# The start of a graph-attention kernel: first rows of h from centred x, first chunk of adj in halves, second group of x inside the units

## The chip, the cores and the metric

The kernel runs on one core of one Trainium2 chip. The metric is device time in microseconds (us), the median of three runs. TensorE is PE in the profile, VectorE is DVE, ScalarE is ACT, GpSimd is POOL and SyncE is SP.

## What is computed

x is 8192 x 128, adj is 8192 x 8192 with zeros and ones, both float32; alpha is 0.5 and beta is 1.

```python
h = jnp.maximum(_layernorm(x, axis=-1), 0.0)
deg = jnp.clip(adj.sum(axis=1), 1.0)
dis = deg ** (-0.5)
diffusion = (dis[:, None] * adj * dis[None, :]) @ h - h
norms = jnp.maximum(jnp.linalg.norm(h, axis=-1), COS_EPS)
sim = h @ h.T / (norms[:, None] * norms[None, :])
attn = jax.nn.softmax(beta * sim * adj, axis=1)
out = x + diffusion + jax.nn.sigmoid(alpha) * (attn @ h - h)
```

## The kernel before

The 8192 rows are 64 tiles of 128. Four groups of 16 tiles (g = 0 to 3) hold x, and later h in its place, in SBUF (`x_st`). The output rows are eight panels of 1024. A unit is one tile of columns against one panel: 512 units, in chunks of 16. For each unit n:

- `cosines(n)` on PE: six matmuls of 512 columns over the halves `uT_hi` and `uT_lo` of the transposed unit rows, into one of two PSUM slots;
- `masked(n)` on DVE (line 718): times the 0/1 bytes of the transposed adj;
- two exponentials on ACT: a half-precision head `ehi` (line 432) and the float32 `ef` (line 436);
- `rest(n)` on POOL (line 339): the tail `elo`;
- `sums(n)` on PE, three units behind (`LAG`): 24 matmuls of 128 or 129 columns.

adj comes from HBM by POOL's queue, cast from float32 to 8 bits on the way: a chunk is four transfers of 32 partitions, each of 1024 rows of 512 elements (2 KB read, 512 B written). Three buffers hold chunks. `turn(m)` (DVE, line 647) transposes a quarter of a chunk, four units' worth, and SP stores the result to HBM for the last stage; `turn(m)` for m >= 4 reuses the place of `turn(m-4)` and is called in unit 4m-3. So chunk 1 is first needed in unit 13, between `masked(13)` and `masked(14)`, and the third quarter of chunk 0 in unit 5.

Ahead of the units: groups 0 and 1 of x are loaded by SP and ACT, then mean and variance of group 0 (`stats_of_x`, `early_var`), a rough reciprocal root on ACT from the float's bits and three Newton steps on DVE (`early_shift`), 16 relu activations on ACT that make h, the squares of h (`stats_of_h`, `square_sums`), a second root (`ssq_root`, `early_norms`), unit rows for the first 16 tiles (eight tiles on DVE, eight on ACT), 16 transposes on PE, and the split of the transposed rows into `uT_hi` and `uT_lo` on DVE (`copy_uT`). PE fills its wait with two blocks of 24 float32 matmuls on the identity (lines 904 and 909; each shows as two passes). Group 1 runs through the same steps in the gaps, its relus ahead of unit 0. Groups 2 and 3 do so in slots of the units given by hand-written tables. In POOL's queue the twelve transfers of chunks 0 to 2 stand first. SP waits for all of chunk 0, then loads groups 2 and 3, then keeps h of groups 0 and 1 in HBM (`keep_h`), and only then stores the turned quarters.

The last stage, from about 1410 us on, is PE's product of the stored adj with the scaled h; the change does not touch it.

Of the kernel before, what the change touches and what calls it, by code (L numbers as in the profile page):

```python
# [5 lines left out]
P = 128  # L6
LN_EPS = 1e-5
# [5 lines left out]
def gnn_block_kernel(nc, x, adj, alpha, beta, out):  # L13
# [27 lines left out]
    WARM = 24  # L41
    LAG = 3
    RS = 3
# [6 lines left out]
    AHEAD = {23: 2, 31: 3, 67: 4, 79: 5, 99: 6, 107: 7}  # L50
# [31 lines left out]
    with ctx:  # L82
# [104 lines left out]
        scalars_ready = sem("scalars_ready")  # L187
        x_loaded = [sem(f"x_loaded{g}") for g in range(CH)]
        vec_chain = sem("vec_chain")
# [51 lines left out]
        def _(sp):  # L241
            sp.dma_start(ab_row[0:1, 0:1], alpha).then_inc(ab_loaded, 16)
            sp.dma_start(ab_row[0:1, 1:2], beta).then_inc(ab_loaded, 16)
# [4 lines left out]
            def keep_h(g):  # L248
                sp.wait_ge(relu_done, 16 * (g + 1))
# [13 lines left out]
            keep_h(1)  # L263
# [5 lines left out]
            for m in range(BLOCKS):  # L269
# [3 lines left out]
                if m in (14, 21):  # L273
                    keep_h(2 if m == 14 else 3)
# [30 lines left out]
        def _(pool):  # L305
# [14 lines left out]


            pool.wait_ge(x_loaded[0], 16 * Q)
            for k in range(RS):
                for part in range(Q):
                    load_rows(k, part)
# [6 lines left out]
            for four in range(4):  # L332
                tail_of_h(four)
# [7 lines left out]
            def first_unit(k):  # L341

                return max(16 * (k - RS) + 13, SUM_UNITS[8 * (k - RS) + 7] + 1)


            tails = {7: 4, 9: 5, 11: 6, 13: 7, 44: 8, 47: 9, 59: 10, 62: 11, 70: 12, 73: 13, 80: 14, 83: 15}
            for n in range(UNITS):
                rest(n)
                if n in tails:
                    tail_of_h(tails[n])  # L350
                for k in range(RS, CHUNKS):
                    part, odd = divmod(n - first_unit(k), 2)
                    if 0 <= part < Q and not odd:
                        if part == 0:
                            pool.wait_ge(rows_summed, 8 * (k - RS + 1))
                            pool.wait_ge(at_ready, W * (k - RS + 1))
                        load_rows(k, part)

        @block.scalar
        def _(act):  # L360
            for g in range(2):
                for q in range(2, Q):
                    act.dma_start(x_st[C * q:C * (q + 1), 16 * g:16 * (g + 1), :].rearrange("c (w b) d -> c w (b d)", b=B),
                                  x_v[g, q]).then_inc(x_loaded[g], 16)
            act.wait_ge(ab_copied, 1)
            nc.scalar.activation(gate_tmp[:, 0:1], ab[:, 0:1], ACT.Exp, scale=-1.0).then_inc(alpha_exp, 1)
# [10 lines left out]

            def relu(g, first, last):
                act.wait_ge(ln_ready, g + 1)
# [4 lines left out]
            def ssq_root(g):  # L384
                of = slice(16 * g, 16 * (g + 1))
                act.wait_ge(hvar_ready, g + 1)
                rough_root(vb[:, of], ssq[:, of]).then_inc(norm_root, 1)

            def head_of_h(hb):
                act.wait_ge(relu_done, 8 * (hb + 1))  # L390
# [33 lines left out]
            act.wait_ge(scalars_ready, 1)  # L424
            for n in range(UNITS):
# [13 lines left out]
                if n in (3, 5, 38, 56, 64, 76):  # L439
                    head_of_h({3: 2, 5: 3, 38: 4, 56: 5, 64: 6, 76: 7}[n])  # L440
                elif n in (7, 55, 87):
                    ssq_root({7: 1, 55: 2, 87: 3}[n])
                elif n in (17, 39):
                    var_root({17: 2, 39: 3}[n])

                if 25 <= n < 49 and n % 3 != 0:
                    relu(2, (n - 25) // 3 * 2 + (n - 25) % 3, (n - 25) // 3 * 2 + (n - 25) % 3 + 1)
                elif 52 <= n < 76 and n % 3 != 0:
                    relu(3, (n - 52) // 3 * 2 + (n - 52) % 3, (n - 52) // 3 * 2 + (n - 52) % 3 + 1)
# [35 lines left out]
        def _(dve):  # L485
# [24 lines left out]
            dve.wait_ge(ab_bcast, 1)  # L510
            link(nc.vector.tensor_copy(ab[:, :], ab_ps))
            link(nc.vector.tensor_scalar(ebias[:, 1:2], ab[:, 1:2], 0.0, -1.0, ALU.max, ALU.mult))
            nc.vector.tensor_scalar(ebias[:, 0:1], ebias[:, 1:2], LN_SCALE, None, ALU.add).then_inc(ab_copied, 1)
            dve.wait_ge(alpha_exp, 1)
            link(nc.vector.tensor_scalar(gate_tmp[:, 1:2], gate_tmp[:, 0:1], 1.0, None, ALU.add))
            link(nc.vector.reciprocal(gate[:, :], gate_tmp[:, 1:2]))
            nc.vector.tensor_scalar(neg_1_gate[:, :], gate[:, :], -1.0, -1.0, ALU.mult, ALU.add).then_inc(scalars_ready, 1)
# [7 lines left out]
            def mean_var(g):  # L525
                for s in range(16):
# [3 lines left out]
            def early_var(g):  # L530
                of = slice(16 * g, 16 * (g + 1))
                link(mean_var(g))
                nc.vector.tensor_scalar(va[:, of], mv[:, of, 1], LN_EPS, None, ALU.add).then_inc(var_ready, 1)

            def early_shift(g):
                of = slice(16 * g, 16 * (g + 1))
                dve.wait_ge(std_ready, g + 1)
                link(refine_root(va[:, of], vb[:, of], vc[:, of], rstd[:, of]))
                nc.vector.scalar_tensor_tensor(out=shift[:, of], in0=mv[:, of, 0], scalar=-1.0, in1=rstd[:, of],
                                               op0=ALU.mult, op1=ALU.mult).then_inc(ln_ready, 1)  # L540

            def stats_of_h(g, first, last):
                dve.wait_ge(relu_done, 16 * g + last)
# [4 lines left out]
            def square_sums(g):  # L548
# [8 lines left out]
                nc.vector.tensor_scalar(ssq[:, of], late_ps[:, 0:16], COS_EPS * COS_EPS, None, ALU.max).then_inc(hvar_ready, 1)  # L557
                dve.wait_ge(hvar_ready, g + 1)

            def early_norms(g):  # L560
                of = slice(16 * g, 16 * (g + 1))
                dve.wait_ge(norm_root, g + 1)
                refine_root(ssq[:, of], vb[:, of], vc[:, of], rnorm[:, of]).then_inc(rnorm_ready, 1)
# [29 lines left out]
            def late_shift(g):  # L593
# [4 lines left out]
                dve.wait_ge(ln_ready, g + 1)  # L598
# [21 lines left out]
            def copy_uT(hb, slot):  # L620
                dve.wait_ge(uT_done, hb + 1)
                of = slice(PW * hb, PW * (hb + 1))
                link(nc.vector.tensor_copy(uT_hi[:, of], cos_ps[:, slot, :]))
# [88 lines left out]
            def masked(n):  # L712
# [3 lines left out]
                if n >= XS:  # L716
# [5 lines left out]
            XSTATS = {6: (2, 0, 4), 7: (2, 4, 9), 8: (2, 9, 10), 9: (2, 10, 11), 11: (2, 11, 12), 12: (2, 12, 13), 13: (2, 13, 14),  # L722
                      14: (2, 14, 16), 24: (3, 0, 1), 25: (3, 1, 2), 27: (3, 2, 3), 28: (3, 3, 4), 29: (3, 4, 5), 30: (3, 5, 6),
                      32: (3, 6, 7), 33: (3, 7, 8), 34: (3, 8, 13), 35: (3, 13, 14), 36: (3, 14, 15), 37: (3, 15, 16)}
            HSTATS = {0: (1, 0, 4), 2: (1, 4, 8), 3: (1, 8, 12), 4: (1, 12, 16),
# [3 lines left out]
            for n in range(UNITS):  # L729
# [16 lines left out]
                if n in (15, 38):  # L746
                    late_var(2 if n == 15 else 3)
                elif n in (19, 20, 21, 41, 42, 43):
                    late_scale(2 if n < 30 else 3, (n - 19) % 22)
                elif n in (22, 45):  # L750
                    late_shift(2 if n == 22 else 3)
                elif n in (6, 54, 86):
                    square_sums({6: 1, 54: 2, 86: 3}[n])
                elif n in (10, 58, 90):
                    for step in range(2):
                        late_norms({10: 1, 58: 2, 90: 3}[n], step)
                elif n in (14, 61, 93):
                    late_norms({14: 1, 61: 2, 93: 3}[n], 2)
                elif n in (18, 26, 62, 70, 94, 102):
# [210 lines left out]
```

## Time and profile before

| | us |
|---|---|
| median of 3 runs | 1862.62 (1861.44 to 1863.44) |
| the profiled execution, its own time | 1862.35 |
| its span in the profile | 1860.2 |
| PE busy | 1829.3 (98%) |
| first `masked` starts | 39.11 |

The span is the profiler's from first to last instruction. PE is busy nearly throughout from the first identity matmul at 22.77 us on; a matmul's end is modelled, so starts are the safer reading.

### The profile page before, as it was taken

Reading aid. Unit: us, or ns where it says so; the run is one execution under the profiler, and the core shown is the slowest. Engines: PE = TensorE matmul, PEld = TensorE weight load, DVE = VectorE, ACT = ScalarE, POOL = GpSimd, SP = SyncE. Lnnn points to the kernel's source line nnn. Section 1 sums busy time; section 2 is a strip of 40 time slices with the busy share of each in tenths; the row PEclk is TensorE's granted clock in tenths of the full one; section 3 lists DMA queues with packets and bytes.
Section 4 is the critical chain, followed back from the end, with each engine's and each line's share of the span. In section 5 each row is a group of like instructions: output and inputs, shape, how many; then the busy total and the mean of one; then the engine's idle time right before and its main releaser. Section 6 shows DMA issues by size and latency. Waiting matters only on the chain.

```text
span 1860.2 us, 44815 instructions
## 1 busy us (share of the span) xinstructions
PE 1829.3 (98%) x19632; PEld 1455.2 (78%) x19632; DVE 1248.2 (67%) x1537; ACT 1272.8 (68%) x1203; POOL 1209.6 (65%) x665
## 2 busy tenths in 40 slices
PE   4999999999999999999999999999999999999999
PEld 4777777777777777777777777777778888888888
DVE  7999899788988777778777877777775211011111
ACT  5989998889888989898988999898986000000000
POOL 3889898889888888888888888888872000000000
PEclk9999999999999999999999999999999999999999
DMA  9967776779978778777677877877337644545520
GB/s 149 191 92 104 113 115 92 102 96 119 118 97 101 104 105 101 109 97 101 92 103 94 101 99 108 101 109 98 111 109 281 227 165 164 193 171 185 201 103 12
DMA packets 188377, 229.39 MB, mean 123 GB/s; under 512 B 5908, under 2 KB 161556, under 8 KB 184084
## 3 DMA queue, kind: packets, MB, share of 16 engines
q0 software_dynamic: 133120, 67.12, 45.5%
q1 hardware_dynamic: 29380, 145.77, 21.4%
q10 hardware_dynamic: 25680, 13.63, 2.7%
q8 instruction: 154, 2.52, 0.5%
q14 instruction: 43, 0.35, 0.0%
HBM read 352.32 MB, written 75.50 MB: 230 GB/s over the span
## 4 chain that ended last, share of the span: by engine, by line
PE 85%; POOL 9%; issue 3%; DVE 1%; ACT 1%; DMA 0%; POOLq 0%; SPq 0%; DVEq 0%; ACTq 0%
PE cos_ps L847 29%; PE cos_ps L930 12%; PE top_ps L930 12%; PE top_ps L893 10%; PE top_ps L897 10%; PE top_ps L895 10%; POOL ustage L339 8%; DVE xe L718 0%; PE cos_ps L904 0%; DMA asb<-x_in 0%; ACT asb L381 0%; ACT xe L436 0%; PE cos_ps L823 0%; POOL arena L318 0%; PE top_ps L909 0%
## 5 line engine op out<-in xcount | busy, mean ns | idle before, releaser
L339 POOL TENSOR_TENSOR ustage<-xe,ustage 128x1024 f16<-128x1024 f32 x512 | 1095.5, 2142 | 177.9 <-ACT xe L436 169.4
L718 DVE TENSOR_TENSOR xe<-cos_ps,arena 128x1024 f32<-128x1024 f32 x512 | 626.5, 1224 | 222.0 <-PE cos_ps L847 135.5
L432 ACT ACTIVATE ustage<-xe,ebias,ab 128x1024 f16<-128x1024 f32 x512 | 635.1, 1241 | 132.5 <-DVE xe L718 131.1
L893 PE MATMUL top_ps<-h,ustage 128*128 128x129 f16 x4096 | 719.0, 220 | 4.9 <-POOL ustage L339 3.6
L897 PE MATMUL top_ps<-h,ustage 128*128 128x129 f16 x4096 | 718.9, 220 | 0.0
L895 PE MATMUL top_ps<-hlo,ustage 128*128 128x128 f16 x4096 | 718.4, 219 | 0.0
L436 ACT ACTIVATE xe<-xe,ebias,ab 128x1024 f32<-128x1024 f32 x512 | 628.7, 1228 | 0.0
L893 PEld LDWEIGHTS top_ps<-h,ustage 128*128 128x128 f16 x4096 | 400.9, 98 | 62.4 <-POOL ustage L339 6.2
L895 PEld LDWEIGHTS top_ps<-hlo,ustage 128*128 128x128 f16 x4096 | 400.8, 98 | 58.0
L897 PEld LDWEIGHTS top_ps<-h,ustage 128*128 128x128 f16 x4096 | 400.8, 98 | 0.0
L654 DVE TENSOR_REDUCE top_ps<-arena 128x8 f32<-128x1024 uint16 x256 | 311.6, 1217 | 0.0
L847 PE MATMUL cos_ps<-uT_hi 128*128 128x512 f16 x1024 | 304.8, 379 | 0.7 <-DVE xe L718 0.6
L847 PE MATMUL cos_ps<-uT_hi,uT_lo 128*128 128x512 f16 x1024 | 304.5, 379 | 0.0
L847 PE MATMUL cos_ps<-uT_lo,uT_hi 128*128 128x512 f16 x1024 | 304.5, 379 | 0.0
L847 PEld LDWEIGHTS cos_ps<-uT_hi,uT_lo 128*128 128x128 f16 x1024 | 116.2, 114 | 104.8
L847 PEld LDWEIGHTS cos_ps<-uT_lo,uT_hi 128*128 128x128 f16 x1024 | 116.1, 113 | 105.0
L647 DVE STREAM_TRANSPOSE arena<-arena 128x1024 uint32<-128x1024 uint32 x128 | 158.0, 1234 | 0.0
L798 DVE SCALAR_TENSOR_TENSOR ptmp<-top_ps,dis,ptmp 128x128 f32<-128x128 f32 x62 | 19.0, 346 | 188.7 <-PE top_ps L930 188.1
L798 DVE SCALAR_TENSOR_TENSOR ptmp<-cos_ps,dis,ptmp 128x128 f32<-128x128 f32 x66 | 20.2, 346 | 160.0 <-PE cos_ps L930 159.4
L318 POOL DMA_DIRECT2D arena<-adj_in_dram x128 | 102.8, 804 | 7.8 <-DMA asb<-x_in 7.8
L930 PE MATMUL cos_ps<-uT_hi,arena 128*128 128x256 f16 x928 | 107.2, 273 | 0.0
L930 PEld LDWEIGHTS cos_ps<-uT_hi,arena 128*128 128x128 fp8e4 x928 | 90.8, 98 | 10.5
(116 smaller groups left out, 1046.8 us busy)
## 6 DMA issues: line engine op xcount, KB each, us to landing
arena<-adj_in_dram POOLq DMA_DIRECT2D x128, 512.0 KB, 10.8
at_scratch<-arena SPq DMA_DIRECT2D x128, 512.0 KB, 5.4
arena<-at_scratch SPq DMA_DIRECT2D x26, 2048.0 KB, 7.9
xe<-at_scratch SPq DMA_DIRECT2D x6, 2048.0 KB, 7.9
h_scratch<-asb SPq DMA_DIRECT2D x16, 256.0 KB, 10.2
arena<-h_scratch SPq DMA_DIRECT2D x16, 256.0 KB, 6.3
ustage<-h_scratch ACTq DMA_DIRECT2D x8, 512.0 KB, 4.1
ptmp<-x_in ACTq DMA_DIRECT2D x8, 512.0 KB, 5.5
```

The source lines that it names most:

```text
L318: pool.dma_start(rows8[k % RS][C * q:C * (q + 1), :, :], adj_v[panel][:, :, 2048 * ch + 512 * q:2048 * ch + 512 * (q + 1)]).then_inc(rows_ ...
L339: nc.gpsimd.tensor_tensor(elo[:, n % ES, :], ef[:, n % XS, :], ehi[:, n % ES, :], ALU.subtract).then_inc(elo_done, 1)
L432: nc.scalar.activation(ehi[:, n % ES, :], xm[:, n % XS, :], ACT.Exp, bias=ebias[:, 0:1], scale=ab[:, 1:2]).then_inc(ehi_done, 1)
L436: nc.scalar.activation(ef[:, n % XS, :], xm[:, n % XS, :], ACT.Exp, bias=ebias[:, 0:1], scale=ab[:, 1:2]).then_inc(ef_done, 1)
L647: nc.vector.transpose(at_words[:, w, :].rearrange("p (a r) -> p a r", r=32), rows_words[k % RS][:, :, 32 * w:32 * (w + 1)]).then_inc(at_re ...
L654: nc.vector.tensor_reduce(out=pairs_ps[:, of], in_=rows_pairs[k % RS][:, 8 * part:8 * (part + 1), :], axis=AX.X, op=ALU.add).then_inc(rows ...
L718: nc.vector.tensor_tensor(xm[:, n % XS, :], cos_ps[:, slot_of(n), :], at8[:, m % W, :, n % B], ALU.mult).then_inc(x_done, 1)
L847: last = nc.tensor.matmul(cos_ps[:, slot_of(n), q * HALF:(q + 1) * HALF].rearrange("p (w z) -> p w z", w=W), own(mine, s), columns(src, pa ...
L893: nc.tensor.matmul(top_ps[:, bank, col:col + P + 1], head, h1[:, s, 0:P + 1], start=(first and t % 3 == 0), stop=final, skip_group_check=True)
L895: nc.tensor.matmul(top_ps[:, bank, col:col + P], head, hlo[:, s, :], start=False, stop=final, skip_group_check=True)
L897: last = nc.tensor.matmul(top_ps[:, bank, col:col + P + 1], tail, h1[:, s, 0:P + 1], start=False, stop=final, skip_group_check=True)
L930: return nc.tensor.matmul(tile_sums(panel, t), slot8[k % SL][:, j // B, t * P:(t + 1) * P, j % B], y[s // 32][:, s % 32, :], start=(s == 0 ...
```

## The change

- Loads: alpha and beta go behind group 0 of x on SP; group 1 is loaded by SP alone, after group 0 has landed. The two small chains on alpha and beta move behind the first unit rows, and into unit 6.
- First rows: a unit row does not depend on the row's scale. Group 0's h is first made without the root, as max(x - mean, 0): eight tiles on ACT, eight on DVE, in place. Squares, root and unit rows follow from that, with the floor of the squares multiplied by the variance. The root of the variance (`first_rstd`) runs on POOL beside it, and h is scaled afterwards, eight tiles on POOL (`scale_first_half`) and eight on ACT (`scale_second_half`). Statistics come in halves of eight tiles.
- The heads `uT_hi` of the first two blocks are copied by ACT (`copy_head`), the tails stay on DVE. The second identity block is 9 instead of 24.
- Group 1: eleven of its 16 statistics stand before unit 0, the rest, its root, relus (units 4 to 16), heads and tails go into the units; groups 2 and 3 move to later slots; the six later transposes of unit rows (`AHEAD`) move to other units.
- Chunk 0 of adj comes as two halves of its columns: each of eight transfers has 1024 rows of 256 elements (1 KB read, 256 B written). `turn(0)` and `turn(1)` need the first half alone. Chunk 1 is issued after `first_rstd`, chunk 2 in units 1, 3, 5 and 7.

```diff
-    AHEAD = {23: 2, 31: 3, 67: 4, 79: 5, 99: 6, 107: 7}
+    AHEAD = {27: 2, 31: 3, 91: 4, 95: 5, 107: 6, 111: 7}
...
-            for g in range(2):
-                load_x(g, 0)
-                load_x(g, 1)
-
+            load_x(0, 0)
+            load_x(0, 1)
+            sp.dma_start(ab_row[0:1, 0:1], alpha).then_inc(ab_loaded, 16)
+            sp.dma_start(ab_row[0:1, 1:2], beta).then_inc(ab_loaded, 16)
+
+            sp.wait_ge(x_loaded[0], 16 * Q)
+            for q in range(Q):
+                load_x(1, q)
             sp.wait_ge(rows_loaded[0], 16 * Q)
...
-                if m in (14, 21):
-                    keep_h(2 if m == 14 else 3)
+                if m in (6, 19, 25):
+                    keep_h({6: 1, 19: 2, 25: 3}[m])
...
+            def load_first_rows(half, q, signal):
+
+                pool.dma_start(rows8[0][C * q:C * (q + 1), :, 256 * half:256 * (half + 1)],
+                               adj_v[0][:, :, 512 * q + 256 * half:512 * q + 256 * (half + 1)]).then_inc(signal, 16)
+
...
+            def first_rstd():
+
+                of = slice(0, 16)
+                pool.wait_ge(std_ready, 1)
+                for step in range(3):
+                    link(nc.gpsimd.tensor_tensor(vc[:, of], va[:, of], vb[:, of], ALU.mult))
+                    link(nc.gpsimd.tensor_tensor(vc[:, of], vc[:, of], vb[:, of], ALU.mult))
+                    link(nc.gpsimd.tensor_scalar(vc[:, of], vc[:, of], -0.5, 1.5, ALU.mult, ALU.add))
...
+            def scale_first_half():
+
+                pool.wait_ge(rstd_ready, 1)
+                pool.wait_ge(u_ready, 1)
+                nc.gpsimd.tensor_tensor(x_st[:, 0:8, :], x_st[:, 0:8, :], rstd[:, 0:8].unsqueeze(2).to_broadcast([P, 8, P]),
+                                        ALU.mult).then_inc(first_scaled, 1)
+
+            first_rstd()
+            for q in range(Q):
+                load_rows(1, q)
+            scale_first_half()
...
-            for four in range(4):
-                tail_of_h(four)
+            tail_of_h(0)
+            tail_of_h(1)
...
-            tails = {7: 4, 9: 5, 11: 6, 13: 7, 44: 8, 47: 9, 59: 10, 62: 11, 70: 12, 73: 13, 80: 14, 83: 15}
+            tails = {2: 2, 4: 3, 13: 4, 15: 5, 20: 6, 23: 7, 60: 8, 63: 9, 74: 10, 77: 11, 88: 12, 91: 13, 98: 14, 101: 15}
...
+            def centred_first_half():
+
+                act.wait_ge(means_ready, 1)
+                for s in range(8):
+                    nc.scalar.activation(x_st[:, s, :], x_st[:, s, :], ACT.Relu, bias=shift[:, s:s + 1]).then_inc(centred, 1)
+
+            def scale_second_half():
+                act.wait_ge(rstd_ready, 1)
+                act.wait_ge(u1_ready, 1)
+                for s in range(8, 16):
+                    nc.scalar.activation(x_st[:, s, :], x_st[:, s, :], ACT.Copy, scale=rstd[:, s:s + 1]).then_inc(second_scaled, 1)
+
...
+            def copy_head(hb):
+                act.wait_ge(uT_done, hb + 1)
+                nc.scalar.activation(uT_hi[:, PW * hb:PW * (hb + 1)], cos_ps[:, hb, :], ACT.Copy).then_inc(uT_head, 1)
+
+            centred_first_half()
             var_root(0)
-            relu(0, 0, 16)
-            var_root(1)
             ssq_root(0)
             second_unit_rows()
+            copy_head(0)
+            copy_head(1)
             head_of_h(0)
-            head_of_h(1)
-            relu(1, 0, 16)
+            act.wait_ge(ab_copied, 1)
+            nc.scalar.activation(gate_tmp[:, 0:1], ab[:, 0:1], ACT.Exp, scale=-1.0).then_inc(alpha_exp, 1)
+            scale_second_half()
...
+            RELU1 = {4: (0, 1), 5: (1, 3), 6: (3, 4), 7: (4, 5), 8: (5, 6), 9: (6, 8), 10: (8, 9), 11: (9, 10), 12: (10, 11), 13: (11, 13),
+                     14: (13, 14), 15: (14, 15), 16: (15, 16)}
...
+                if n in (1, 11, 17, 57, 71, 85, 95):
+                    head_of_h({1: 1, 11: 2, 17: 3, 57: 4, 71: 5, 85: 6, 95: 7}[n])
+                elif n in (18, 84, 99):
+                    ssq_root({18: 1, 84: 2, 99: 3}[n])
+                if n in (1, 38, 54):
+                    var_root({1: 1, 38: 2, 54: 3}[n])
...
+            def centred_second_half():
+                for s in range(8, 16):
+                    last = nc.vector.tensor_scalar(x_st[:, s, :], x_st[:, s, :], shift[:, s:s + 1], 0.0, ALU.add, ALU.max)
+                link(last)
...
-            stats_of_x(0, 0, 16)
-            early_var(0)
-            early_shift(0)
-            stats_of_x(1, 0, 16)
-            early_var(1)
-            for four in range(4):
-                stats_of_h(0, 4 * four, 4 * (four + 1))
+            for half in range(2):
+                stats_of_x(0, 8 * half, 8 * (half + 1))
+                first_means(half)
+            first_var()
+            centred_second_half()
+
+            dve.wait_ge(ab_bcast, 1)
+            for half in range(2):
+                stats_of_h(0, 8 * half, 8 * (half + 1))
             square_sums(0)
-            early_norms(0)
+            first_norms()
             first_unit_rows()
-            early_shift(1)
+            exp_scalars()
+            stats_of_x(1, 0, 8)
             copy_uT(0, 0)
+            stats_of_x(1, 8, 11)
             copy_uT(1, 1)
...
-                if w == 0:
+                if m == 0:
+                    dve.wait_ge(rows_first, 16 * Q)
+                elif m == 2 or k and w == 0:
                     dve.wait_ge(rows_loaded[k % RS], 16 * Q * (k // RS + 1))
...
+                if n in (2, 38, 54):
+                    late_var({2: 1, 38: 2, 54: 3}[n])
+                elif n in (3, 42, 58):
                     for step in range(2):
-                        late_norms({10: 1, 58: 2, 90: 3}[n], step)
...
-            pe.wait_ge(relu_done, 16)
+            pe.wait_ge(centred, 8)
             for k in range(WARM):
                 nc.tensor.matmul(cos_ps[:, 0, 0:P], ident32[:, :], ident32[:, :], start=True, stop=True)
             transposed(0, 0)
             transposed(1, 1)
 
-            for k in range(WARM):
+            for k in range(KEPT_WARM):
```

## Rows read from the trace of the kernel before

**Rows 1.** Busy time of the engines in two stretches (us from the span's start).
```profile
core 0: us, PE busy (x) PEld busy (x) DVE busy (x) ACT busy (x) POOL busy (x), PEclk, DMA share, GB/s
...
40.00:80.00 40.00, 38.19 (x413) 27.95 (x412) 36.91 (x79) 38.26 (x35) 34.34 (x19) 1.00 1.16 217
...
400.00:440.00 40.00, 40.00 (x453) 30.39 (x451) 35.03 (x34) 35.91 (x31) 35.40 (x20) 1.00 0.76 103
```

**Rows 2.** Timeline of 9 to 31 us: start, duration, engine, line, operation, count.
```profile
9.29 3.19 DVE L522 BATCH_NORM_STATS2 ptmp<-asb 128x6 f32<-128x128 f32 x16 [2.95 <-DMA asb<-x_in]
9.59 9.38 POOL L318 DMA_DIRECT2D arena<-adj_in_dram  x12 [7.81 <-DMA asb<-x_in]
12.52 1.17 DVE L527 BATCH_NORM_AGGREGATE mv<-ptmp 128x2 f32<-128x6 f32 x16
...
13.93 0.31 ACT L371 ACTIVATE vb<-va,bits_bias 128x16 f32<-128x16 int32 x1 [8.15 <-DVE va L533]
...
16.36 6.26 ACT L381 ACTIVATE asb<-asb,shift,rstd 128x128 f32<-128x128 f32 x16 [2.12 <-DVE shift L539]
...
20.75 3.62 DVE L545 BATCH_NORM_STATS2 top_ps<-asb 128x6 f32<-128x128 f32 x16
...
24.40 0.19 DVE L552 COPY ptmp<-top_ps 128x32 f32<-128x32 f32 x1
...
25.51 0.31 ACT L371 ACTIVATE vb<-ssq,bits_bias 128x16 f32<-128x16 int32 x1 [2.68 <-DVE ssq L557]
...
27.80 1.23 DVE L608 TENSOR_TENSOR xe<-asb,rnorm 128x1024 f32<-128x1024 f32 x1
27.81 2.45 ACT L396 ACTIVATE xe<-asb,rnorm 128x128 f32<-128x128 f32 x8 [1.99 <-DVE rnorm L498]
```

**Rows 3.** Timeline of 22 to 40 us, around the transposes and the first unit.
```profile
22.77 7.83 PE L904 MATMUL cos_ps<-ident 128*128 128x128 f32 x48 [17.81 <-ACT asb L381]
...
30.44 1.91 PE L823 MATMUL cos_ps<-ident,xe 128*128 128x128 f32 x16
...
31.51 1.23 DVE L623 CAST uT_hi<-cos_ps 128x1024 f16<-128x1024 f32 x1 [0.51 <-PE cos_ps L823]
...
32.18 5.52 PE L909 MATMUL top_ps<-ident 128*128 128x128 f32 x48
...
36.30 1.23 DVE L647 STREAM_TRANSPOSE arena<-arena 128x1024 uint32<-128x1024 uint32 x1
...
39.11 1.22 DVE L718 TENSOR_TENSOR xe<-cos_ps,arena 128x1024 f32<-128x1024 f32 x1 [1.58 <-PE cos_ps L847]
```

**Rows 4.** Timeline inside the units: POOL, PE and ACT at the start.
```profile
42.88 8.93 POOL L339 TENSOR_TENSOR ustage<-xe,ustage 128x1024 f16<-128x1024 f32 x4 [7.23 <-ACT xe L436]
...
44.98 1.23 ACT L432 ACTIVATE ustage<-xe,ebias,ab 128x1024 f16<-128x1024 f32 x1
...
45.08 0.23 PE L893 MATMUL top_ps<-h,ustage 128*128 128x129 f16 x1 [1.16 <-POOL ustage L339]
...
49.51 1.04 ACT L391 ACTIVATE h<-asb 128x1024 f16<-128x1024 f32 x1
...
62.74 1.12 POOL L330 TENSOR_TENSOR hlo<-asb,h 128x512 f16<-128x512 f32 x1
```

**Rows 5.** Timeline of DVE in unit 13: the mask, then the first quarter of chunk 1.
```profile
71.99 1.23 DVE L718 TENSOR_TENSOR xe<-cos_ps,arena 128x1024 f32<-128x1024 f32 x1
73.13 1.24 DVE L647 STREAM_TRANSPOSE arena<-arena 128x1024 uint32<-128x1024 uint32 x1
```

**Rows 6.** DMA queues of 3 to 9, 12 to 32, 32 to 69, 45 to 50, and 96 to 110 us, in this order.
```profile
DMA packets 788, 1.44 MB, mean 240 GB/s; under 512 B 84, under 2 KB 84, under 8 KB 788
...
q0 software_dynamic: 4046, 2.05, 123.3%
...
q0 software_dynamic: 4110, 2.07, 66.2%
q1 hardware_dynamic: 2830, 6.15, 48.4%
...
q1 hardware_dynamic: 504, 0.91, 54.7%
...
q1 hardware_dynamic: 220, 0.84, 15.2%
```

More of the change, by code:

```diff
@@ L41, in gnn_block_kernel @@
     WARM = 24
+    KEPT_WARM = 9
     LAG = 3
@@ L186, in gnn_block_kernel @@
         alpha_exp = sem("alpha_exp")
-        scalars_ready = sem("scalars_ready")
         x_loaded = [sem(f"x_loaded{g}") for g in range(CH)]
+        rows_first = sem("rows_first")
+        means_ready = sem("means_ready")
+        centred = sem("centred")
+        root_chain = sem("root_chain")
+        rstd_ready = sem("rstd_ready")
+        first_scaled = sem("first_scaled")
+        second_scaled = sem("second_scaled")
+        uT_head = sem("uT_head")
         vec_chain = sem("vec_chain")
@@ L248, in keep_h @@
             def keep_h(g):
-                sp.wait_ge(relu_done, 16 * (g + 1))
+                if g == 0:
+                    sp.wait_ge(first_scaled, 1)
+                    sp.wait_ge(second_scaled, 8)
+                else:
+                    sp.wait_ge(relu_done, 16 * g)
                 for q in range(Q):
@@ L350, in _ @@
                     tail_of_h(tails[n])
-                for k in range(RS, CHUNKS):
+                for k in range(RS - 1, CHUNKS):
                     part, odd = divmod(n - first_unit(k), 2)
                     if 0 <= part < Q and not odd:
-                        if part == 0:
+                        if part == 0 and k >= RS:
                             pool.wait_ge(rows_summed, 8 * (k - RS + 1))
@@ L360, in _ @@
         def _(act):
[L361 to L366, printed above, removed]
+            for q in range(2, Q):
+                act.dma_start(x_st[C * q:C * (q + 1), 0:16, :].rearrange("c (w b) d -> c w (b d)", b=B), x_v[0, q]).then_inc(x_loaded[0], 16)
+            act.wait_ge(consts_ready, 1)
+            nc.scalar.activation(gz[0:1, 0:1], ones32[0:1, 0:1], ACT.Exp)
             def rough_root(root, value):
@@ L523, in stats_of_x, with mean_var, first_means, first_var @@
                 link(ins)
-            def mean_var(g):
-                for s in range(16):
+            def mean_var(g, first=0, last=16):
+                for s in range(first, last):
                     ins = nc.vector.bn_aggr(out=mv[:, 16 * g + s, :], in_=stats[:, s, :])
                 return ins
[L530 to L540, printed above, removed]
+            def first_means(half):
+                of = slice(8 * half, 8 * (half + 1))
+                link(mean_var(0, 8 * half, 8 * (half + 1)))
+                minus = nc.vector.tensor_scalar(shift[:, of], mv[:, of, 0], -1.0, None, ALU.mult)
+                if half == 0:
+                    minus.then_inc(means_ready, 1)
+                else:
+                    link(minus)
+            def first_var():
+                nc.vector.tensor_scalar(va[:, 0:16], mv[:, 0:16, 1], LN_EPS, None, ALU.add).then_inc(var_ready, 1)
+            def centred_second_half():
+                for s in range(8, 16):
+                    last = nc.vector.tensor_scalar(x_st[:, s, :], x_st[:, s, :], shift[:, s:s + 1], 0.0, ALU.add, ALU.max)
+                link(last)
             def stats_of_h(g, first, last):
-                dve.wait_ge(relu_done, 16 * g + last)
+                if g:
+                    dve.wait_ge(relu_done, 16 * (g - 1) + last)
+                elif first == 0:
+                    dve.wait_ge(centred, last)
                 for s in range(first, last):
@@ L597, in late_shift @@
                                                op0=ALU.mult, op1=ALU.mult).then_inc(ln_ready, 1)
-                dve.wait_ge(ln_ready, g + 1)
+                dve.wait_ge(ln_ready, g)
             def late_norms(g, step):
@@ L745, in _ @@
                     stats_of_h(*HSTATS[n])
[L746 to L754, printed above, removed]
-                    for step in range(2):
-                        late_norms({10: 1, 58: 2, 90: 3}[n], step)
-                elif n in (14, 61, 93):
-                    late_norms({14: 1, 61: 2, 93: 3}[n], 2)
-                elif n in (18, 26, 62, 70, 94, 102):
-                    late_unit_rows({18: 2, 26: 3, 62: 4, 70: 5, 94: 6, 102: 7}[n])
+                if n in (2, 38, 54):
+                    late_var({2: 1, 38: 2, 54: 3}[n])
+                elif n in (3, 42, 58):
+                    for step in range(2):
+                        late_scale({3: 1, 42: 2, 58: 3}[n], step)
+                elif n in (4, 43, 59):
+                    late_scale({4: 1, 43: 2, 59: 3}[n], 2)
+                elif n in (5, 44, 60):
+                    late_shift({5: 1, 44: 2, 60: 3}[n])
+                elif n in (18, 84, 99):
+                    square_sums({18: 1, 84: 2, 99: 3}[n])
+                elif n in (22, 102):
+                    for step in range(2):
+                        late_norms({22: 1, 102: 3}[n], step)
+                elif n in (87, 88):
+                    late_norms(2, n - 87)
+                elif n in (23, 89, 103):
+                    late_norms({23: 1, 89: 2, 103: 3}[n], 2)
+                elif n in (26, 30, 90, 94, 106, 110):
+                    late_unit_rows({26: 2, 30: 3, 90: 4, 94: 5, 106: 6, 110: 7}[n])
+                elif n == 6:
+                    gate_scalars()
                 elif n == 186:
```

94 lines of the change are left out of this document (55 added, 39 removed), and 9 rows, old and new, of tables (HSTATS, XSTATS).

## The prediction

> **What bounds the kernel now.** I read first the busy time by stretches [rows 1]. From 400 us on PE starts 453 matmuls in 40 us; a unit has 30, so a unit costs 2.65 us and PE has no idle time. From 40 to 80 us it starts 413, so the start-up is looser. Whatever happens on the other engines in a steady unit is hidden as long as it fits in 2.65 us; what the change can win is the time before unit 0, and what it can lose is PE idle time in the units that now carry more work. The timeline gives the clock of the start: group 0 of x has landed at 9.29 [rows 2], the first mask starts at 39.11 [rows 3], the first `sums` at 45.08 after a wait for POOL [rows 4], and mask 13 at 71.99 [rows 5]. From the first `sums` on PE is packed: mask 13 follows mask 0 by 32.88 us. The DMA queues are the third view [rows 6]: they are busy from 2 us to beyond 69 us, so they are a second chain beside the engines.
>
> **The start, step by step.** I write T for the landing of group 0. Before, T = 9.29 with 2.1 MB of x in flight. The queues move 240 GB/s at this time [rows 6]; 1.05 MB takes 4.4 us, from about 2 us on, and the last packets need about 1.3 us more to be seen (before, the slower queue had moved its share of group 0 at about 8). So T falls to 7.7, a gain of 1.6.
>
> From T on, with the costs of [rows 2]: eight statistics at 0.20, eight aggregates at 0.073 and a negation of 0.2 give the first means at T+2.45, the second at T+4.85, the variance at T+5.05. ACT centres eight tiles at 0.39 from T+2.45 to T+5.6. DVE centres the other eight; no row shows this operation, the nearest are 0.13 (half of 0.25) and 0.23 (a statistic written to PSUM); I take 0.20, ending at T+6.65. Then 16 statistics of h at 0.226 (T+10.3), the squares 1.1 (from 24.40 to 25.51), the rough root 0.4, nine Newton steps from about 25.9 to 27.8, so 1.9: the norms are there at T+13.7. Before it was 27.80 - 9.29 = 18.5. The first root with its Newton steps (13.93 to 16.36, 2.4 us) is gone from the path, and the 16 relus one after the other (6.3) are shared by two engines. Gain 4.8. The root now on POOL (14 dependent small operations; at 0.15 to 0.5 each they take 2 to 7 us, ready by T+13 at the latest) is covered by the squares; without that cover its excess would delay chunk 1's issue and the scaling of h, not the unit rows.
>
> After the norms: DVE's unit rows to T+14.9, ACT's to T+16.2 (1.23 and 2.45, [rows 2]). Eight transposes take 0.95 [rows 3]. Before, they were late for the identity block, which ran from 22.77 to 30.6 though the rows stood at 29.03; now this block begins with the centred tiles at T+5.6 and is over at T+13.5. ACT copies the first head T+16.2 to 17.4 and the second to T+18.6 (1.04 to 1.24 each, [rows 3, 4]); DVE meanwhile does the scalars (0.6), eight statistics (1.6), the first tail to T+18.6, three statistics, the second tail to T+20.4, and `turn(0)` to T+21.6. The nine kept identity matmuls take 9/24 of 5.52, so 2.1, and end at T+19.3, before the first cosines. Cosines at T+20.4 and 1.6 us until the mask can start: T+22.1 = 29.8. Before it took 11.3 from norms to mask, now 8.4: gain 2.9. In all the mask of unit 0 moves from 39.11 to 29.8, **9.3 us earlier**.
>
> **What the units pay.** POOL's order in units 0 to 7 was eight `rest` at 2.14; now four DMA issues of 0.78 (9.38/12, [rows 2]) and two tails of 1.1 [rows 4] stand between them: 22.6 us against PE's 21.2. ACT's unit 1 now has a head (1.0) and the root of group 1, for which it waits until DVE's `late_var` in unit 2 (mask 2, then 16 aggregates and two small ones, 1.6): ACT starts unit 2 about 7.4 us after mask 0, where before it was 5.87 (44.98, [rows 4]), and `rest(2)` starts some 1.0 late for that. Followed unit by unit against PE at 2.65 from the first `sums`, elo is latest in unit 6, by POOL's 1.4 and ACT's 1.0, 2.4 us together. I charge **2.4**; bounds 0.8 (POOL alone, the load behind ACT's wait) and 5. ACT's relus in units 4 to 16 (16 at 0.39 beside two exponentials at 1.14, 2.66 a unit) just keep pace; the head and the state copy at units 17 and 18 cost up to 0.9 where before a like bubble stood at unit 16. Later slots of groups 2 and 3 change places, not number; the six extra transposes stay six. I set these at 0, within 1 either way. The end is untouched.
>
> **What the DMA pays.** Before, chunk 0 ran alone from 12.0 (2.4 after its issue at 9.59) to 32: 4046 packets in 20 us, 0.078 us of one of the 16 DMA engines per 2 KB packet (20 x 16 / 4096). Chunk 1 was through at 69, in 37 us: 20 of its own and 16.9 for 6.15 MB on SP's queue, 2.75 us per MB [rows 6]. It was needed at 73.13 [rows 5]: only 4 us of slack. Now it must be there for mask 14 at 29.8 + 32.9 + 2.4 = 65.1 for mask 13, and PE has three units of work in hand: `turn(4)` and mask 14 in front of cosines 16, and the exponentials and `rest(14)` (6.0 after the mask) in front of `sums(14)`, allow the chunk to come as late as 65.1 + 3.5 = 68.6. In its way are: start at 7.7 + 2.4 = 10.1; chunk 0 in 8192 packets of 1 KB read and 256 B written; chunk 1, 20 us; group 1 of x, groups 2 and 3, h of group 0 alone (h of group 1 moved to unit 21) and four stores of 0.52 MB, 6.3 MB less 0.3 moved before 10.1, 16.5 us. Chunk 1 lands at 46.6 + 512 c, with c the price of a small packet in us. No row shows such packets. By bytes read alone c = 0.039, by packets alone 0.078. The raw times of SP's packets are 0.087 at 1.8 KB (54.7% of 80 engine-us, 504) and 0.155 at 3.8 KB [rows 6]; on their line 1 KB is 0.060, and with the overlap of this queue (0.078 for 0.0975 raw) 0.048. Most of the price is bytes; I take 0.045. Chunk 1 lands at 69.6: **1.0 of stall**. At 0.039 it is 66.6 and hidden. SP's first store waits behind twelve transfers as before, but lands before chunk 1 and does not decide. The halves themselves: the first lands at 10.1 + 11.5 + 2.4 for group 1 = 24.5, needed at 28.1; the second at 36, needed about 43.
>
> **Sum.** 9.3 - 2.4 - 1.0 = 5.9 us. The profiled execution took 1862.35, the median of the runs is 1862.62, within 0.02%. Forecast 1862.35 - 5.9 = **1856.5**.
>
> **The rivals.**
> 1. *Small packets cost as much as large ones* (c = 0.078). The first half lands at 32.5, the second at 53, chunk 1 at 86.5, 17.9 after the limit; 9.3 - 2.4 - 17.9 = -11.0, so 1873.4. This is the case on the other side: place, `turn(4)`; it decides from c = 0.055 on, where the stall of 6.2 leaves 0.7. For it speaks that POOL's queue moves the same 200 packets per us or fewer whatever stands beside it; against it that 3.8 KB packets take 1.8 times as long as 1.8 KB ones. The Trainium skill, DMA: Bandwidth & Descriptors, section Specifications, says that 512 B is the least transfer for line rate and that below it the DMA engine reads, modifies and writes; by that rule the 256 B writes would lie on this rival's side, and no row here shows them. Chance 0.13, and 0.12 for prices between (c 0.052 to 0.065: 1860 to 1867).
> 2. *The units pay more*: POOL and ACT late by 5 instead of 2.4, as bubbles of DVE, ACT and POOL add up rather than overlap. 1859 to 1862. For it speaks that ACT and POOL have 0.4 and 0.5 us of slack per unit. Chance 0.13.
> 3. *Nothing is late*: PE takes `sums` early enough, chunk 1 lands at 66.6. 1862.35 - 9.3 = 1853. Chance 0.10.
> 4. *The start isn't shorter*: group 0 alone lands no earlier and the centred steps cost double. Then 9.3 shrinks to 5, the rest with it: 1860. Chance 0.04.
>
> **How the numbers follow.** The forecast's case (1854 to 1859.5) has 0.48. The range reaches from 1853 to 1868: below lie 0.05, above 0.13 of the chance. 0.2% is 3.7 us, about what this kernel's measurement can tell from no change; faster by more means under 1858.9: 0.43 of the forecast's case, rival 3, and a part of rivals 2 and 4, 0.60. Slower means over 1866.3: rival 1 and the upper end of the prices between, 0.18. Same, 0.22.
>
> **What would show it.** Mask 0 at about 29.8, group 0 of x at 7.7, norms at 21.4. POOL's queue: packets of chunk 0 through at 36, chunk 1 at 69.6. In unit 13 the wait of `turn(4)`, a few us on chunk 1's landing; over 8 us means rival 1. PE's waits for POOL in units 3 to 8 together 2 to 3 us. Mask 140 is to come 5.9 us before its old time. Wrong would make it above all the packet price, next a wait of ACT on DVE in unit 1 that I have undersized.

## The result, and the profile after

The changed kernel takes **1873.51 us** (1872.08 to 1873.87, 4 runs), the one before 1862.38 in the same job: ratio 1.0058 (95% interval 1.0046 to 1.0070), 11.1 us slower where 5.9 faster was forecast. The span of its profile is 1872.0, 11.8 longer than before. Executions of one kernel differ here by up to 3.3 us, so where it matters the single ones are named below.

The start went as worked out. The timeline of the changed kernel, to the first mask:

```profile
6.83 1.64 DVE L601 BATCH_NORM_STATS2 ptmp<-asb 128x6 f32<-128x128 f32 x8 [4.13 <-DMA asb<-x_in]
...
20.61 0.17 DVE L574 SCALAR_TENSOR_TENSOR rnorm<-vc,vb 128x16 f32<-128x16 f32 x1
...
29.11 1.22 DVE L822 TENSOR_TENSOR xe<-cos_ps,arena 128x1024 f32<-128x1024 f32 x1 [0.50 <-PE cos_ps L959]
```

Group 0 has landed at 6.83, the norms stand at 20.8 and mask 0 starts at 29.11, 10.0 us before the old one [rows 3]. What follows gives back more than that. Starts of the same masks in the two timelines, in us:

| mask | before | after | after less before |
|---|---|---|---|
| 0 | 39.11 | 29.11 | -10.0 |
| 13 | 71.99 | 64.70 | -7.3 |
| 18 | 85.67 | 80.89 | -4.8 |
| 26 | 108.57 | 105.73 | -2.8 |
| 31 | 123.40 | 125.70 | +2.3 |
| 90 | 282.35 | 283.75 | +1.4 |
| 115 | 350.55 | 362.35 | +11.8 |
| 130 | 390.28 | 402.07 | +11.8 |

From unit 115 on nothing changes any more. The account in masks closes: of the 10.0 us at mask 0, 2.7 are gone by mask 13, 2.5 more by mask 18 and 3.1 more by mask 20; between masks 20 and 130 the changed kernel needs 312.44 us and the old one 298.96, which is 13.5 more. The list of PE's waits in the changed kernel (who waited for whom, us in total, times, longest) names the place:

```profile
PE cos_ps L935 <- DVE ptmp L711: 10.6, 6, 2.6
...
PE top_ps L1005 <- POOL ustage L390: 4.7, 7, 1.1
PE cos_ps L959 <- DVE xe L822: 2.6, 2, 1.9
PE top_ps L1005 <- ACT asb L493: 2.2, 1, 2.2
```

Line 935 is the transpose of unit rows, line 711 their making in `late_unit_rows`. Six waits are the six transposes of `AHEAD`. One of them, on DVE and PE around unit 27:

```profile
105.73 1.23 DVE L822 TENSOR_TENSOR xe<-cos_ps,arena 128x1024 f32<-128x1024 f32 x1
...
107.07 1.22 DVE L711 TENSOR_TENSOR ptmp<-asb,top_ps 128x1024 f32<-128x1024 f32 x1
...
108.43 1.06 PE L935 MATMUL cos_ps<-ident,ptmp 128*128 128x128 f32 x8 [1.65 <-DVE ptmp L711]
...
109.60 1.22 DVE L721 CAST uT_hi<-cos_ps 128x1024 f16<-128x1024 f32 x1 [1.32 <-PE cos_ps L935]
...
110.86 1.22 DVE L722 TENSOR_TENSOR uT_lo<-cos_ps,uT_hi 128x1024 f16<-128x1024 f32 x1
...
112.00 1.21 DVE L822 TENSOR_TENSOR xe<-cos_ps,arena 128x1024 f32<-128x1024 f32 x1
```

Mask 26, unit rows, transposes, head, tail, mask 27 stand one behind another across two engines: 6.27 us between masks, where a unit has 2.65. The two tables say why (`AHEAD`, and the one of `late_unit_rows`): unit rows are made in units 26, 30, 90, 94, 106, 110, and the transposes come in 27, 31, 91, 95, 107, 111, one unit later each time. Before, they were made in 18, 26, 62, 70, 94, 102 for 23, 31, 67, 79, 99, 107, five to nine units ahead. The excess over 2.65 of the six mask distances is 22.2 us in the changed kernel and 11.5 in the old one: 10.7 more.

The DMA side came out nearly at the forecast times, in part by errors that cancel (below). Queue q0 of 20 to 30 us, which then carries chunk 0's small packets alone, and DVE around unit 13:

```profile
DMA packets 3914, 0.99 MB, mean 99 GB/s; under 512 B 3914, under 2 KB 3914, under 8 KB 3914
```

```profile
64.70 1.22 DVE L822 TENSOR_TENSOR xe<-cos_ps,arena 128x1024 f32<-128x1024 f32 x1 [0.45 <-DVE top_ps L632]
69.98 1.25 DVE L751 STREAM_TRANSPOSE arena<-arena 128x1024 uint32<-128x1024 uint32 x1 [4.05 <-DMA arena<-adj_in_dram]
```

3914 packets in 10 us are 0.041 us of a DMA engine each, against 0.078 for a packet of 2 KB read and 512 B written [rows 6]: a packet of half the bytes costs half. The trace has the landing of each transfer: the last of chunk 0's first half at 24.88 (forecast 24.5), of its second half at 35.51 (36), of chunk 1 at 69.95 (69.6). `turn(4)` waits 4.05 us for it and starts at 69.98. In the old kernel chunk 1 landed at 71.26. So the whole change of the transfers brought chunk 1 forward by 1.3 us, while its reader came 7.3 us earlier.

A third loss was not in the forecast at all: the pause at unit 20 and the clock behind it. PE by stretches in the changed kernel (busy time, instructions, granted clock):

```profile
82.00:84.00 2.00, 0.83 (x4) 1.00 1.24 104
84.00:86.00 2.00, 0.94 (x14) 0.91 1.13 293
86.00:88.00 2.00, 2.00 (x16) 0.50 1.21 107
88.00:90.00 2.00, 2.00 (x17) 0.74 1.25 110
```

PE idles for more than half of 82 to 86 us (it waits 2.2 us for ACT's copy of the sums, line 493), and its granted clock then falls from 1.00 to 0.50, that is from 2.4 to 1.2 GHz. The same follows the pause before unit 91 (0.50 in 288 to 290 us). Over 84 to 90 the missing clock is worth 0.18 + 1.0 + 0.52 = 1.7 us. The old kernel keeps 1.00 in all its units. The Trainium skill, TensorE: Matmul & The Clock Gate, Part 1, names these two levels, with the low one for an idle array; the trace agrees on the levels, and both falls come behind a wait of PE (2.2 and 2.6 us).

### The profile page after: what moved, and what is told of

Read it like the earlier page. It is cut to its first block, busy times and chain, and to the rows that moved or that the text cites. A ratio compares the mean times of both kernels' runs of the same rounds, so it can differ in the third digit from the quotient of the medians.

```text
span 1872.0 us, 44790 instructions
## 1 busy us (share of the span) xinstructions
PE 1833.0 (98%) x19602; PEld 1453.0 (78%) x19602; DVE 1246.6 (67%) x1538; ACT 1273.0 (68%) x1206; POOL 1217.1 (65%) x682
## 4 chain that ended last, share of the span: by engine, by line
PE 81%; POOL 11%; DVE 4%; issue 4%; ACT 0%; DMA 0%; POOLq 0%; DVEq 0%; ACTq 0%
PE cos_ps L959 28%; PE cos_ps L1042 12%; PE top_ps L1042 12%; POOL ustage L390 10%; PE top_ps L1005 10%; PE top_ps L1009 10%; PE top_ps L1007 9%; DVE xe L822 1%; POOL arena L331 0%; DVE top_ps L758 0%; DVE ptmp L711 0%; DVE arena L751 0%; PE cos_ps L935 0%; DVE ptmp L601 0%; DMA asb<-x_in 0%
```

## The experiments

Times are medians; the kernel before, in the jobs of these runs, took 1862.64, 1862.21 and 1862.60. A difference between medians of two jobs is less sure than one between two masks of the traces, so both are given where it matters.

**Unit rows further from their transposes.** In the changed kernel:

```diff
-    AHEAD = {27: 2, 31: 3, 91: 4, 95: 5, 107: 6, 111: 7}
+    AHEAD = {27: 2, 31: 3, 93: 4, 98: 5, 109: 6, 113: 7}
...
-                    late_unit_rows({26: 2, 30: 3, 90: 4, 94: 5, 106: 6, 110: 7}[n])
+                    late_unit_rows({24: 2, 28: 3, 90: 4, 95: 5, 106: 6, 110: 7}[n])
```

> The changed kernel, with each late unit-row step moved three units ahead of the transposes that read it (it stood one unit ahead). Theory S, spacing: the six transposes stall PE because their rows are made one unit before; 10.7 us of the loss is this, so the time falls from 1873.5 to about 1863, and masks 27, 31, 93, 98, 109 and 113 follow their forerunners by 4.1 to 4.6 us, not 6.3. Theory D, DMA: the loss is the late chunk 1 and its after-effects; the time stays at 1870 or above.

Measured: 1863.58 us (10 runs), ratio to before 1.0006 (0.9997 to 1.0016). PE's waits for unit rows are gone from the list:

```profile
PE top_ps L1005 <- POOL ustage L390: 4.7, 7, 1.1
PE cos_ps L959 <- DVE xe L822: 4.2, 5, 1.8
PE cos_ps L935 <- DVE xe L703: 2.9, 1, 2.9
PE cos_ps L959 <- DVE uT_lo L722: 2.7, 3, 1.0
```

The line 935 that is left is the first pair of transposes, ahead of unit 0. The two tables cost 9.9 us of the 11.1 by the medians. By the traces, masks 20 to 130 take 303.4 us instead of 312.4, so 9.0 less, and still 4.4 more than in the old kernel. The profile is of the slowest of the ten executions (1865.72): its clock fell once more ahead of unit 0, at 22.1, behind a wait of 2.9 us, and mask 0 came at 30.10 for 29.11.

The distance of masks at units 27 and 31 is 3.53, less than expected; at 93, 98, 109 and 113 it is 4.6 to 5.0, more than expected. But where the rows for 27 and 31 are made, in units 24 and 28, the next mask is 1.4 us late as well (4.05 for 2.65). Together that is 1.4 + 0.9 = 2.3 us for one set of eight tiles, about what the other four cost at the transposes alone (2.0 to 2.4).

**The same from the other side.** In the kernel before, only this:

```diff
-                elif n in (18, 26, 62, 70, 94, 102):
-                    late_unit_rows({18: 2, 26: 3, 62: 4, 70: 5, 94: 6, 102: 7}[n])
...
+                if n in (22, 30, 66, 78, 98, 106):
+                    late_unit_rows({22: 2, 30: 3, 66: 4, 78: 5, 98: 6, 106: 7}[n])
```

> The kernel before, with nothing changed but the late unit-row steps, moved from four to twelve units ahead of their transposes to one unit ahead. Theory S: about 10 us slower, 1872 to 1873, each of the six transposes costing 3.6 to 4.1 us of mask distance above 2.65. Theory D and others: within 2 us of before, as the DVE work is the same.

Measured: 1875.21 us, ratio 1.0068 (1.0053 to 1.0083), 12.6 us slower; 10 were expected. The six distances are 6.3 to 6.7 us, 3.6 to 4.0 above the 2.65 of a unit, as expected, and masks 20 to 130 take 12.5 us longer than before. One fall of the clock to 0.50 stands in that, at 125.1 behind a wait of 2.1 us; the expectation had none. The list of waits has the new line, and DVE's timeline the gap before the head:

```profile
PE cos_ps L823 <- DVE ptmp L616: 9.7, 6, 2.4
```

```profile
97.97 1.22 DVE L616 TENSOR_TENSOR ptmp<-asb,top_ps 128x1024 f32<-128x1024 f32 x1
100.51 1.23 DVE L623 CAST uT_hi<-cos_ps 128x1024 f16<-128x1024 f32 x1 [1.31 <-PE cos_ps L823]
```

One table moved in an otherwise untouched kernel costs more than the whole change lost. Together with the run before, this settles the main cause.

**Chunk 0 whole**, in the changed kernel:

```diff
-            for q in range(Q):
-                load_first_rows(0, q, rows_first)
-            for q in range(Q):
-                load_first_rows(1, q, rows_loaded[0])
+            for q in range(Q):
+                load_rows(0, q)
...
-                if m == 0:
-                    dve.wait_ge(rows_first, 16 * Q)
-                elif m == 2 or k and w == 0:
+                if w == 0:
```

> The changed kernel with chunk 0 loaded whole, in four transfers with 512 B written per packet, and turn 0 waiting for all of it. Mask 0 starts about 5.5 us later (34.5 for 29.1). If small packets cost what their bytes cost (0.041 us), chunk 1 lands within 1 us of 70 as before and the time stays within 1.5 us of 1873.5: the halves win nothing because turn 4 takes it back. If small packets cost as much as large ones, chunk 1 lands up to 20 us earlier and the time falls by 4 us or more.

Measured: 1877.10 us, ratio 1.0075 (1.0059 to 1.0092), 3.6 slower than the changed kernel. DVE's waits:

```profile
DVE arena L747 <- DMA arena<-adj_in_dram: 7.3, 1, 7.3
```

Mask 0 starts at 35.38, 6.3 later, and `turn(4)` waits no more: masks 13 and 14 are 2.60 apart. Of the 6.3 us that the halves win in front, 3.6 are left at mask 18, so the wait of `turn(4)` takes 2.7 back. "Within 1.5" was too low, but small packets as dear as large ones are refuted here too: chunk 1 lands at 68.75, only 1.2 us before its landing in the changed kernel and not up to 20, and the time did not fall. PE waits 7.0 us for mask 0 in this run, and the granted clock is 0.50 from 31.9 to 42.1 us; masks 0 and 13 are 35.60 apart all the same, as in the changed kernel (35.59).

**Group 3 of x behind the fifth store**, in the changed kernel:

```diff
-            for g in range(2, CH):
-                for q in range(Q):
-                    load_x(g, q)
+            for q in range(Q):
+                load_x(2, q)
             keep_h(0)
...
+                if m == 4:
+                    for q in range(Q):
+                        load_x(3, q)
```

> The changed kernel with the load of group 3 of x (1.05 MB) moved from ahead of chunk 1 to behind the fifth store. Chunk 1 should land 2.9 us earlier, at about 67, and turn 4's wait fall from 4.1 to about 1. Theory S: 1 to 3 us gained, 1871 to 1872.5. Theory D: the stall is the main loss, 1868 or less.

Measured: 1871.05 us, ratio 1.0045 (1.0030 to 1.0060), 2.5 less than the changed kernel. The four executions took 1869.76, 1870.06, 1872.03 and 1872.26.

```profile
DVE arena L753 <- DMA arena<-adj_in_dram: 2.4, 1, 2.4
```

The wait is 2.4 for 4.05, and mask 18 comes at 79.25 for 80.89. About 1 was expected: chunk 1 lands at 68.3, not at 67. Mask 130 is 1.8 earlier, as is the profiled execution (1872.03 for 1873.87), so the rest of the 2.5 is the scatter of the executions. The stall at `turn(4)` is real, what is taken from it passes to the end in full, and it is the smaller part.

**Both groups later, with the rows apart.** The first experiment's kernel, with `load_x(2, ...)` at m = 3 and `load_x(3, ...)` at m = 5.

> The changed kernel with the unit rows three units ahead (as in the run before) and groups 2 and 3 of x loaded behind the fourth and sixth store, out of the way of chunk 1. Theory: the queue is 5.8 us lighter in front of chunk 1, turn 4 waits under 1 us (4.0 before), and mask 15 comes about 6 us ahead of the old kernel's, where it was 3.2. Time 1863.6 - 3 = 1860 to 1861. Rival: the wait moves to a later load or store (groups 2 and 3 late for their statistics in unit 20 and 46) and nothing is gained, 1863 or more.

Measured: 1862.33 us, ratio 0.9999 (0.9990 to 1.0008), 1.25 less than with the rows apart alone; 3 were expected. The wait of `turn(4)` is still 1.9:

```profile
DVE arena L751 <- DMA arena<-adj_in_dram: 1.9, 1, 1.9
```

The reason can be read from the order: the fourth store goes out in unit 9, some 15 us before chunk 1 is through, so group 2 still shares the queues with it and only group 3 is out of the way. The expectation counted both. The run showed something else. Mask 20 follows mask 19 by 4.31 us here, by 5.84 with group 3 alone moved and the same wait of 2.2 for ACT; the granted clock tells them apart, first the run with group 3 alone moved, then this one:

```profile
82.00:84.00 2.00, 0.58 (x6) 0.80 1.15 246
84.00:86.00 2.00, 2.00 (x22) 0.50 1.18 154
86.00:88.00 2.00, 2.00 (x16) 0.84 1.24 109
```

```profile
82.00:84.00 2.00, 1.20 (x22) 1.00 1.09 289
84.00:86.00 2.00, 2.00 (x22) 1.00 1.14 234
86.00:88.00 2.00, 2.00 (x24) 1.00 1.14 237
```

One fall of the clock costs 1.5 us. The eleven executions of this one kernel lie in two groups: five took 1860.5 to 1861.0 us with a mean granted clock of 0.999 to 1.000, six took 1862.3 to 1862.8 with 0.998 to 0.999. The profile is of the first group. Their mean clocks fit one fall in each execution of the second group, of which no trace was kept. So the forecast of 1860 to 1861 holds for the first group, and the median tells which group was larger. PE waited 2.2 us in both profiles; what decides whether the clock falls behind such a wait is not shown.

**POOL's issues and ACT's head.** Added to the run before: `return 8 if k < RS` for `return 1`, and head 3 in unit 19 for 17.

> The kernel of the run before, and in it POOL's four issues for chunk 2 moved from units 1 to 7 to units 8 to 14, and ACT's head of tiles 24 to 31 from unit 17 to 19, behind the copy of the sums. Theory: the start-up units lose 2.7 us because POOL is on the chain there with four issues of 0.8 and two tails, and 1 us at unit 20 because the head stands in front of the copy; 1 to 2.5 us less than the run before. Rival: ACT or DVE holds the same units anyway, under 0.5 us.

Measured: 1860.08 us, ratio 0.9989 (0.9980 to 0.9998), 2.25 less. All eleven executions lie between 1859.75 and 1860.77, by their medians 0.8 below the first group of the run before, where 1 to 2.5 were expected; the rest of the 2.25 is the second group, which is gone. In the traces mask 130 is 0.5 earlier, though here too the clock fell once ahead of unit 0 (at 21.7, behind a wait of 2.9 us) and made mask 0 0.6 later. Mask 13 follows mask 0 by 34.84 instead of 35.60, and PE's wait for the copy of the sums is 0.6 for 2.2:

```profile
PE top_ps L1005 <- ACT asb L493: 0.6, 1, 0.6
```

**Even units.** Added to that: transposes in units 30, 38, 94, 100, 110, 118, unit rows in 26, 34, 90, 95, 106, 114.

> The kernel of the run before, with the six transposes moved again: four to five units behind their unit rows and five of them into units that are even (DVE has neither a quarter to turn nor, mostly, rows to sum there). Theory: at three units PE waits no more for the unit rows, but DVE's split of the transposed rows (2.4 us) still stops the masks in a full unit, 2.0 to 2.3 us each where the old kernel lost 1.0 to 1.9; with light units 1 to 3 us less than the run before. Rival: the cost is the eight transposes and the shared slot, wherever they stand: within 0.7 us.

Measured: 1862.22 us, ratio 0.9998 (0.9989 to 1.0007), 2.1 more than the run before. The executions lie in two groups again, five at 1860.7 to 1861.2 and six at 1862.2 to 1862.9, and the profile, of the second, has a fall of the clock at 309.6, behind a wait of 2.0 us in unit 100. Even the first group is 0.7 above the run before. The theory failed: the distances at the transposes are 4.6 to 6.1, no less. What did get cheaper is the making of rows in unit 26 (masks 26 to 27: 2.65), where rows in units 24 and 28 had cost 1.4 each.

**Five units apart.** The changed kernel, with only this and two bundles of statistics moved out of units 34 and 98:

```diff
-    AHEAD = {27: 2, 31: 3, 91: 4, 95: 5, 107: 6, 111: 7}
+    AHEAD = {31: 2, 39: 3, 95: 4, 103: 5, 111: 6, 119: 7}
...
-                    late_unit_rows({26: 2, 30: 3, 90: 4, 94: 5, 106: 6, 110: 7}[n])
+                    late_unit_rows({26: 2, 34: 3, 90: 4, 98: 5, 106: 6, 114: 7}[n])
```

> The changed kernel, only with its late transposes placed anew: unit rows in units 26, 34, 90, 98, 106, 114 (of the form 4k+2, in which DVE neither turns nor sums), transposes five units later, in units of the form 4k+3, and two bundles of statistics shifted out of the units of the rows. Theory: the transposes then cost what they cost the old kernel, 0.9 to 1.2 us each, where three units of distance in units with a turn or a sum cost 2.0 to 2.3 and the rows 1.4: 1859 to 1861, against 1863.6 at distance three and 1873.5 at distance one. Rival: only the distance matters and the kind of unit doesn't, 1863 to 1864.

Measured: 1862.08 us, ratio 0.9997 (0.9989 to 1.0006): 11.4 less than the changed kernel and 1.5 less than three units apart. Better than the rival's 1863, short of the forecast. Masks 20 to 130 take 301.7 us for 303.4, which is 1.7 less and free of falls of the clock in both traces, so the placement gains that much; distance and kind of unit were changed together, and no run separates them. In the units its profile has one fall of the clock, behind the wait of `turn(4)`:

```profile
72.00:74.00 2.00, 0.64 (x3) 1.00 1.24 109
74.00:76.00 2.00, 2.00 (x11) 0.52 1.21 173
76.00:78.00 2.00, 2.00 (x22) 0.63 1.13 227
```

**All together.** This placement with groups 2 and 3 later, POOL's issues in units 8 to 14 and the head in unit 19.

> The kernel of the run before with groups 2 and 3 of x behind the fourth and sixth store, POOL's issues for chunk 2 in units 8 to 14 and ACT's head in unit 19. Theory: the three gains add (5 for the placement, 3 for turn 4, 1.5 for POOL and ACT): 1854.5 to 1857, the first version that is clearly under the old kernel. Rival: the last units before 120 carry too much work and the placement gains under 2: 1858 to 1860.

Measured: **1858.18 us** (1857.91 to 1858.78, 10 runs), ratio 0.9978 (0.9969 to 0.9987). This beats the old kernel by 4.4 us and the changed one by 15. It is 1.2 above the expected range and in the rival's. The placement was to give 5 us and gave 1.9 against three units apart (1860.08), and 1.55 between masks 20 and 130; whether the full last units hold it back, as the rival says, no run tests. Of the 10.2 us at mask 0, 2.0 are gone at mask 13, 1.4 more at mask 20 and 2.9 more at mask 130, so that 3.9 are left.

**All together, chunk 0 whole.**

> The kernel of the run before with chunk 0 whole. Mask 0 comes 5 us later (34.5), since turn 0 waits for 20 us of packets instead of 10. Theory: with turn 4 off the path the delay stays to the end, 4 to 5.5 us above the run before. Rival: chunk 1 decides still and the halves are worth under 2 us.

Measured: 1864.79 us, ratio 1.0011 (1.0002 to 1.0020), 6.6 above the run before, where 4 to 5.5 were expected; mask 0 is 6.7 later (35.62 for 28.95), where 5 were. `turn(4)` still waits 1.9 us in the run before and not here, but by mask 18 the difference is 6.75 again: the short wait was made good, and all that the halves win stays won.

## Why the prediction was wrong

The step that failed is the last one of what the units pay: "Later slots of groups 2 and 3 change places, not number; the six extra transposes stay six. I set these at 0, within 1 either way." The number stayed, the distance between making the rows and transposing them did not. It cost 9.9 us (taken away) and 12.6 (put into the old kernel), more than the whole difference to the old kernel's time in the second case. The other half of the sentence was wrong as well, "Later slots of groups 2 and 3 change places": with the rows three units ahead, masks 20 to 130 still take 4.4 us more than in the old kernel, and 2.9 in the best version. What of the new slots costs that is open. Both tables stood in the code; the prediction asked how many transposes there are, not how far each stands from its rows.

- **The start**: right. 9.3 forecast, 10.0 measured; group 0 landed at 6.83 for 7.7, the norms followed 13.9 later for 13.7. POOL's root was twelve small operations, not fourteen, and took 3.6 us (13.49 to 17.07).
- **The first units**: the size right. 2.4 forecast, 2.7 measured between masks 0 and 13. That POOL's issues are part of it is shown by the move to units 8 to 14 (0.8 of it). ACT was nearer its limit than the prediction says: 16 relus of 0.39 in 13 units beside two exponentials of 1.14 are 2.76 us a unit, not 2.66, and that is more than PE's 2.65. That this makes up the other 1.9 is not shown.
- **The DMA**: the landing right (69.95 for 69.6), in part by luck. At the measured price of 0.041 for 0.045 the prediction's own sum gives 67.6, in time; something else cost the 2.4 us between. One error is a reading: chunk 1 was not "through at 69" before the change but landed at 71.26, 1.9 us ahead of its reader at 73.13 and not 4. (The first half of chunk 0, 10.1 + 11.5 + 2.4, is 24.0 and not 24.5; nothing hangs on it.) The tolerance was wrong too. Mask 13 came at 64.70, so the prediction's rule (3.5 us behind it) puts the limit at 68.2 and the stall at 1.8. Between masks 13 and 18 the kernel lost 2.5, and taking 1.6 us from the wait gave 1.8 back. A likely reason, not shown, is that the reserve of three units was partly used up: PE had waited 2.3 us for POOL in units 2 to 8 already.
- **Unit 20 and the clock**: missing. The head in front of the copy of the sums was priced at up to 0.9 and set at 0; PE's wait rose from 0.7 to 2.2, and the clock fell behind it, 1.5 more.
- **Rival 1** gave 1873.4, the measured time to 0.1 us, by luck, and is refuted all the same: its packets cost 0.041, not 0.078, and chunk 1 landed at 69.95, not at 86.5. The Trainium skill's rule of 512 B as the least transfer for line rate (DMA: Bandwidth & Descriptors, Specifications) is not borne out for these 256 B writes into SBUF behind 1 KB reads: their packets took 0.041 us where 0.078 was paid for twice the bytes. Bytes read and bytes written were halved together, so no run tells which of them sets the price.

Still open is where the best version loses 2.9 us between masks 20 and 130 (its six distances at the transposes are 1.1 longer together, the rest is in other slots), what decides whether the clock falls, and which part of the 3.4 us that the best version loses before mask 20 is group 1's work in the units.

## What to carry to other kernels

When a hand-written table of slots is changed, look at each pair of producer and consumer and count the units between them: here a producer one unit ahead of its reader made each of six units 3.6 us longer or more, and the same work five to nine units ahead 1.4 to 2.7. A gain in front of a pipeline must be followed to the end of all that it makes denser; here 10 us at the first unit became 11.8 us lost by unit 115, and 4.4 gained once three waits were loosened. When executions of one kernel fall into two groups, compare groups and traces before medians: 1.5 us or more of some differences here was the clock. And a forecast time that comes true proves nothing about its mechanism; only the row that the mechanism names does.

## What the hardware showed

- Small packets of POOL's queue, 1 KB read and 256 B written, go at 391 per us (3914 in 10 us), those of 2 KB and 512 B at 202 (4046 in 20 us, [rows 6]).
- Short pauses of PE can cost more than their length. Behind waits of 2.0 to 2.6 us in the units the granted clock fell from 1.00 to 0.50 in seven of the kernels' traces, at 1.5 us of delay where two traces can be compared. Behind others of the same length it stayed at 1.00 (2.2 us with groups 2 and 3 both moved, 2.4 us in the first transpose of the old kernel with its rows moved), and in one kernel, by the mean clocks, about half of the executions had a fall and the others none. So a wait of 2 us is a risk of 1.5 more, and not a fixed price.
